# Adding routed expert outputs onto the residual stream in memory, by a scatter with addition

## What is computed

```python
x = x + attention(layer_norm(x))                  # 12 heads of 16
xn = layer_norm(x).reshape(4096, 192)
logits = xn @ gate_w                              # 8 experts
top_logits, top_idx = top_k(logits, 2)
top_gates = softmax(top_logits)                   # two weights for each token
y_e = gelu(xn @ w1[e] + b1[e]) @ w2[e] + b2[e]    # hidden size 768
return x + sum over the two chosen e of gate_e * y_e
```

## Time and profile before

| | us |
|---|---|
| median of 3 runs | 2392.24 |
| lowest and highest | 2391.66, 2395.35 |
| span of the profiled execution | 2403.1 |
| of it, from the first load of the last stage to the end | 29.7 |

### The profile page before, as it was taken

One profiled execution on the slowest core, in us unless ns is written; L12 is line 12 of the kernel. 1 busy time (PEld: TensorE's weight loads), 2 busy tenths in 40 slices (PEclk: granted clock), 3 DMA queues, 4 the chain that ended last, 5 costly groups with the idle time before them and its releaser, 6 DMA issues. The chain is left out here.

```text
span 2403.1 us, 30974 instructions
## 1 busy us (share of the span) xinstructions
PE 1879.3 (78%) x9780; PEld 1007.5 (42%) x9804; DVE 1495.5 (62%) x2518; ACT 1074.7 (45%) x1896; POOL 395.9 (16%) x595
## 2 busy tenths in 40 slices
PE   3868788858876453777668877998899984999994
PEld 2745655535333320000022234442133333888883
DVE  4558449966010687999878876999788883111114
ACT  1100222214110476999979964342477661222220
POOL 5000000000112010222100003331033343222221
PEclk8989999968887575555589978997799996999997
DMA  3011110005797004443011008777666703566664
GB/s 85 1 39 31 48 31 27 20 10 229 309 411 314 20 0 127 127 127 123 18 32 40 26 16 119 130 132 107 83 88 95 97 28 135 195 201 203 202 203 184
DMA packets 147792, 264.98 MB, mean 110 GB/s; under 512 B 28864, under 2 KB 115985, under 8 KB 142678
## 3 DMA queue, kind: packets, MB, share of 16 engines
q1 hardware_dynamic: 135750, 242.10, 38.0%
q0 software_dynamic: 10768, 18.19, 2.3%
q10 hardware_dynamic: 1152, 3.15, 0.3%
HBM read 221.85 MB, written 57.71 MB: 116 GB/s over the span
## 5 line engine op out<-in xcount | busy, mean ns | idle before, releaser
L1743 PE MATMUL ps<-arena 128*128 x376 | 194.9, 621 | 108.2 <-ACT ps L1785 60.1
L1785 ACT ACTIVATE ps<-ps,arena 128x512 f32<-128x512 f32 x384 | 256.7, 1121 | 6.3 <-POOL arena L1769 6.3
L1753 DVE TENSOR_REDUCE arena<-ps 128x1024 f32 x192 | 232.8, 1225 | 24.5 <-PE ps L1743 12.2
L1785 ACT ACTIVATION_READ_ACCUMULATOR ps<-ps,arena 128x1 f32 x384 | 234.7, 668 | 0.0
L2159 DVE TENSOR_REDUCE arena<-ps 128x1024 f32 x192 | 221.3, 1219 | 12.4 <-PE ps L2405 9.8
L2618 ACT ACTIVATE arena<-ps 128x1024 f32<-128x1024 f32 x192 | 185.1, 1020 | 97.6 <-PE ps L2500 96.4
L2962 DVE TENSOR_TENSOR arena<-ps,arena 128x384 f32<-128x384 f32 x39 | 21.8, 558 | 286.4 <-PE ps L2918 286.4
L2942 ACT ACTIVATE arena<-ps,arena 128x256 f32<-128x256 f32 x234 | 89.5, 481 | 235.9 <-PE ps L2907 230.0
L2405 PE MATMUL ps<-arena 96*128 96x512 bf16 x500 | 162.7, 430 | 26.4 <-DVE arena L2159 12.2
L1950 ACT ACTIVATE arena<-ps 128x1024 f32<-128x1024 f32 x192 | 178.7, 1048 | 7.8 <-DVE arena L1970 4.6
L529 PE MATMUL ps<-arena 96*128 96x456 f32 (+1 forms) x512 | 170.3, 482 | 8.8 <-DMA arena<-la_xt 5.2
(11 more groups left out here) (394 smaller groups left out, 3264.8 us busy)
## 6 DMA issues: line engine op xcount, KB each, us to landing
arena<-in_sm_w_dram SPq DMA_DIRECT2D x128, 576.0 KB, 15.5
arena<-in_re_w_dram SPq DMA_DIRECT2D x39, 1252.0 KB, 5.9
arena<-ra_parts SPq DMA_DIRECT2D x192, 192.0 KB, 9.1
routed_in<-routed_in SPq DMA_DIRECT2D x8, 3332.0 KB, 14.2
ra_parts<-arena SPq DMA_DIRECT2D x48, 192.0 KB, 2.4
arena<-routed_in SPq DMA_DIRECT2D x39, 196.0 KB, 5.4
arena<-la_xt SPq DMA_DIRECT2D x16, 384.0 KB, 3.4
arena<-arena SPq DMA_DIRECT2D x64, 96.0 KB, 2.2
```

The lines of the kernel that those rows point to most:

```text
L1743: ins = pe.matmul(ps[:, 2 * (n % 4) + t % 2, :], QM[j][:, h, t * P:(t + 1) * P], KI[:, b, h // HG, :], start=True, stop=True)
L1753: v.tensor_reduce(MXq[:, b, 2 * u:2 * u + 2, at_head(h)], ps[:, 2 * (n % 4):2 * (n % 4) + 2, :], AX.X, ALU.max).then_inc(s_lk, 1)
L1785: ins = act.activation(bank, bank, ACT.Exp, bias=nb[n % 4][:, t % 2:t % 2 + 1], scale=c_reg, accum_out=RS[:, b, t, at_head(h):at_head(h) + 1])
```

## The change

1. The gate weights are made batch by batch. `best_two` also takes the logit gap of its batch (DVE, L2711 of the changed kernel). ACT takes its exponential in `gap_exp(b - 2)`, behind score unit e = 3 of batch b. DVE makes the two weights in `gates`, right behind `places`.
2. `send` copies the weight into word 1 of each row's header on POOL (it waits for `gates`), and word 0 is now the token's own row number, the same for both of its rows.
3. SP stores each batch of the stream `m.H`, as soon as it holds the attention output, into a new DRAM array `routed_sum` (`keep_stream`).
4. In the expert stage DVE also copies the weights from the header, and multiplies `YM` by them with two instructions. POOL's indirect DMAs add onto `routed_sum` instead of storing into `routed_out`.
5. The last stage only copies `routed_sum` to the output, DRAM to DRAM, four copies from SP's and four from ACT's queue. The 16 loads and 64 DVE instructions are gone.

```diff
+            def keep_stream(p):
+                sp.wait_ge(s_hs, p + 1)
+                sp.dma_start(io.routed_sum[p * S:(p + 1) * S].rearrange("(p t) d -> p t d", t=T), m.H[:, p, :, :]
+                             ).then_inc(m.sums_set, 16)
...
+                if b > 2:
+                    keep_stream(b - 3)
...
+            keep_stream(B - 3)
+            keep_stream(B - 2)
             av.wait(sp, B - 1, NS)
...
                 load_rows(sp, io, m, n, at[n])
+            keep_stream(B - 1)
...
+            def gap_exp(p):
+                act.wait_ge(s_d, p + 1)
+                act.activation(gap[p % 2], gap[p % 2], ACT.Exp).then_inc(s_e, 1)
...
+                    if b > 1 and e == 3:
+                        gap_exp(b - 2)
...
+            gap_exp(B - 2)
             turned_copy(B - 1, 0, 0)
             turned_copy(B - 1, 1, 2)
+            gap_exp(B - 1)
...
                 if b and not last:
                     places(b - 1)
+                    gates(b - 1)
...
+                best = VM[:, p * T:(p + 1) * T, :]
+                v.tensor_tensor(gap[p % 2], best[:, :, 1], best[:, :, 0], ALU.subtract).then_inc(s_d, 1)
...
+            def gates(p):
+
+                v.wait_ge(s_e, p + 1)
+                first, second = GT[p % 2][:, 0, :], GT[p % 2][:, 1, :]
+                gate(v.tensor_scalar(second, gap[p % 2], 1.0, None, ALU.add))
+                gate(v.reciprocal(first, second))
+                v.tensor_tensor(second, first, gap[p % 2], ALU.mult).then_inc(s_gt, 1)
...
-                pool.iota(to_row[a], [[1, T]], base=k * NT * P + p * S, channel_multiplier=T).then_inc(s_ir, 1)
-                pool.wait_ge(s_ir, 2 * p + k + 1)
+                pool.iota(to_row[a], [[1, T]], base=p * S, channel_multiplier=T).then_inc(s_ir, 1)
+                pool.wait_ge(s_gt, p + 1)
+                pool.tensor_copy(XA[a][:, :, 1], GT[p % 2][:, k, :]).then_inc(s_ir, 1)
+                pool.wait_ge(s_ir, 2 * (2 * p + k + 1))
...
-                yc.wait(pool, n, 1)
+                yw.wait(pool, n, 1)
...
-                                            YM[j][:, h, :], None).then_inc(m.ym[j], 16)
+                                            YM[j][:, h, :], None, compute_op=ALU.add).then_inc(m.ym[j], 16)
...
+                v.tensor_copy(weight[n % 4], XM[n % 2][:, :, 1])
...
+                yc.wait(v, n, 1)
+                for h in range(2):
+                    ins = v.tensor_scalar(YM[n % 2][:, h, :], YM[n % 2][:, h, :], weight[n % 4][:, h:h + 1], None,
+                                          ALU.mult)
+                ins.then_inc(yw.sem, 1)
...
-                        ins = v.scalar_tensor_tensor(out=m.H[:, b, t, :], in0=Y[:, b, k, t, :],
-                                                     scalar=GT[:, T * b + t, k:k + 1], in1=m.H[:, b, t, :],
-                                                     op0=ALU.mult, op1=ALU.add)
...
+        def copy_out(eng, batches):
+            for b in batches:
+                eng.dma_start(io.out[b].rearrange("(p t) d -> p (t d)", t=T),
+                              yd[b * S:(b + 1) * S].rearrange("(p t) d -> p (t d)", t=T)).then_inc(s_o, 16)
```

More of the change, by code:

```diff
@@ L2031, in routed_attention @@
     m.TE, m.TID = gx(P, [NTILE], I32), gx(P, [NTILE], I32)
-    m.GT, d = gx(P, [B * T, 2]), gx(P, [B * T])
+    GT, gap = [gx(P, [2, T]) for _ in range(2)], [gx(P, [T]) for _ in range(2)]
     to_row = [a.bitcast(I32)[:, :, 0] for a in XA]
@@ L2458, in routed_attention @@
         SG("rows_turned_copied", 2), SG("logits"), SG("logits_copied"), SG("masks"), SG("ranks"), SG("places")
-    s_gl, s_gb, s_ir, s_d, s_e, s_te = (sem(f"ra_gate_{n}") for n in (
-        "chain", "rows_scaled", "return_rows_set", "gap", "gap_exp", "tile_tables"))
+    s_gl, s_gb, s_ir, s_d, s_e, s_te, s_gt, s_hs = (sem(f"ra_gate_{n}") for n in (
+        "chain", "rows_scaled", "headers_set", "gap", "gap_exp", "tile_tables", "gates", "stream_summed"))
     s_sc = [nc.alloc_semaphore(f"ra_rows_sent{k}") for k in range(2)]
@@ L2677, in logits @@
             def logits(p, bank):
-                v.tensor_tensor(m.H[:, p, :, :], m.H[:, p, :, :], X[p % 2], ALU.add)
+                v.tensor_tensor(m.H[:, p, :, :], m.H[:, p, :, :], X[p % 2], ALU.add).then_inc(s_hs, 1)
                 if p == B - 1:
@@ L2742, in _ @@
             places(B - 2)
+            gates(B - 2)
             add_projection(B - 1, (7, 3), True)
@@ L2749, in _ @@
             places(B - 1)
+            gates(B - 1)
             gate(v.tensor_tensor(row0, row0, part0, ALU.subtract))
@@ L2768, in _ @@
             v.tensor_scalar(m.TID, TG, float(NX * PART), None, ALU.min).then_inc(s_te, 1)
-            v.tensor_tensor(d, VM[:, :, 1], VM[:, :, 0], ALU.subtract).then_inc(s_d, 1)
-            v.wait_ge(s_e, 1)
-            gate(v.tensor_scalar(m.GT[:, :, 1], d, 1.0, None, ALU.add))
-            gate(v.reciprocal(m.GT[:, :, 0], m.GT[:, :, 1]))
-            gate(v.tensor_tensor(m.GT[:, :, 1], m.GT[:, :, 0], d, ALU.mult))
         @block.gpsimd
@@ L2837, in routed_experts @@
 def routed_experts(nc, m, io):
-    ps, GT, WR, wl = m.ps, m.GT, m.WR, m.wl
-    xd, yd = io.routed_in, io.routed_out
+    ps, WR, wl = m.ps, m.WR, m.wl
+    xd, yd = io.routed_in, io.routed_sum
     sem = lambda name: SEMS.new(nc, name)
@@ L2845, in routed_experts @@
     XM, XT, HT, YM = m.XM, two([2, TR]), two([KH, TR]), two([2, D])
-    back = [w(P, [2], I32) for _ in range(4)]
+    back, weight = [w(P, [2], I32) for _ in range(4)], [w(P, [2]) for _ in range(4)]
     xm = m.xm
@@ L2849, in routed_experts @@
     S2 = lambda n, per=1: Signal(nc, f"re_t_{n}", per, 2 * per)
-    xt, xc, hp, gl, yp, yc, yf = S2("rows_turned"), S2("rows_turned_copied"), S2("hidden", 3), S2("gelu", 3), \
-        S2("out"), S2("out_copied"), S2("out_buffer_free")
+    xt, xc, hp, gl, yp, yc, yw, yf = S2("rows_turned"), S2("rows_turned_copied"), S2("hidden", 3), S2("gelu", 3), \
+        S2("out"), S2("out_copied"), S2("out_weighted"), S2("out_buffer_free")
     unit = lambda k: ps[:, 1 + k, 0:TR]
@@ L2948, in _ @@
             yc.start(v)
+            yw.start(v)
             def rows(n):
```

35 lines of the change are left out of this document (9 added, 26 removed).

## The result

| | before | changed |
|---|---|---|
| median, us | 2392.48 | 2417.72 |
| lowest and highest, 4 runs each | 2391.66, 2395.35 | 2411.17, 2423.11 |
| span of the profiled execution | 2403.1 | 2409.4 |

The ratio is 1.0094, 95% interval 1.0075 to 1.0113: 22.5 us slower (18 to 27), or 25.2 by the medians. The forecast was 2398.4 with a range up to 2412. The sign was right and the size was not.

The account below looks back on a forecast made before the run. PE and DVE, both near full, were taken to bound the attention loop by hand-overs, PE the expert loop, and DVE sums the last stage. 14.6 + 3.6 + 1.8 - 13.8 = +6.2 us gave 2398.4 us; range 2392 to 2405, wider 2386 to 2412.

Parts of the forecast that it names:

- ACT's wait: Attention loop, behind unit 3: ACT waits for DVE's gap in six batches, making the kernel 14.6 us slower in sum.
- PE's clock: Rival, attention loop: PE's clock falls in the new pauses, adding 9.9 us, to 2408.3; chance 0.14.
- The rival's price: Attention loop, clock rival: 2.15 us more for a batch at low clock, 9.9 us in all; chance 0.14.
- Gates: Attention loop, DVE between the ranks and step 8: three small instructions, 0.6 us a batch, 3.6 us loss.
- The offset between profile and median: Whole kernel: the profiled execution was 10.9 us over the median before, taken as the same after.
- Free wait (rival): Attention loop: batches settle with MAX8 ahead of unit 3, the wait costs nothing, 2385.0 us; chance 0.14.
- Between the stages: Between attention and expert loops: last gap and gates, POOL's copies and last stream store lose 1.8 us, ends 0.8 and 3.
- Expert loop: Expert stage: DVE's 0.8 us more in each tile is hidden and landing may grow by 5.7 us, so no loss.
- Tail: Last stage: 8 DRAM to DRAM copies of 13.0 us replace loads and DVE sums, gain 13.8 us, ends 7.7 and 17.9.

Follow-up runs that it names:

- E9: The changed kernel with fourteen matmuls that nobody reads put into TensorE's pause behind unit 3: ratio 1.0070 to the kernel before, six batches 227.4 us.
- E10: The changed kernel, exponential still behind unit 3, with only the gates moved into VectorE's idle time: ratio 1.0062 to the kernel before, six batches 225.8 us.
- E4: The changed kernel without gap subtraction, exponential, gates and weight copy, so expert outputs are unweighted: ratio 0.9933 to the kernel before, six batches 203.3 us.
- E2: The changed kernel with the exponential behind unit 7 and the gates moved into VectorE's idle time: ratio 0.9928 to the kernel before, tail 21.3 us.
- E7: E2 with GpSimd's scatters storing instead of adding, which changes the computation: ratio 0.9922 to the kernel before, tail 18.3 us.
- E8: E2 with stream and experts' rows put straight into the output, padding beyond the scatter's bound, no last stage: ratio 0.9895 to the kernel before.
- E1: The changed kernel with ScalarE's small exponential moved from behind unit 3 to behind unit 7: ratio 0.9968 to the kernel before, six batches 206.1 us.
- E3: The kernel before plus only the gap subtraction and its exponential behind unit 3, result unused: ratio 1.0060 to the kernel before, six batches 226.2 us.
- E5: The changed kernel with ScalarE's small exponential behind unit 5 instead of unit 3: ratio 0.9975 to the kernel before, six batches 211.7 us.
- E6: The changed kernel with eight matmuls that nobody reads put into TensorE's pause behind unit 3: ratio 1.0043 to the kernel before, six batches 230.4 us.

## Why the prediction was wrong, step by step

- **ACT's wait: right.** Foreseen 3.6 us late in four batches, 3.2 and 3.6 in the others; measured 3.9 in six. The rest is that the exponential starts behind the gap. The price that the forecast derived by following the queue, 2.9 us a batch, is 2.8 in the batches at full clock of E9 and 3.1 in that of E10.
- **PE's clock: the step that failed.** The forecast carried the wait through at the speed of the kernel before ("when PE alone sets the pace") and kept the low clock as a rival with a chance of 0.14 and a price of 9.9 us. The runs take the 34.8 us apart: E4, which has neither wait nor gates, has 203.3 us for the six batches, 2.2 less than the kernel before (E2, E7 and E8 have the same loop and spread over 4 us, so each of these numbers is good to some 2); gates add 2.8 (E1, 206.1); the bare wait adds 6 x 2.8 = 17; and the 17 that are left up to 240.3 are half clock (19.5 if counted as 240.3 - 6 x 36.8). The forecast named alone, and there the low clock did not follow a pause: PE had stood for no more than 0.3 us in the 8 us before. The row that bears on a pause stands elsewhere in the kernel before, in its timeline of PE at 735 us:

```profile
734.97 0.88 PE L1259 MATMUL ps<-arena 4*128 4x384 f32 x2 [3.55 <-issue]
735.77 0.85 PE L1262 MATMUL ps<-arena 128*32 128x384 f32 x8
736.56 1.64 PE L1259 MATMUL ps<-arena 4*128 4x384 f32 x2
```

Behind 3.55 us of idleness two matmuls of L1259 take 0.88 us, and the next two of the same line, at half clock, 1.64 us; the granted clock is 1.00 before, 0.62 from 736 to 738 us and 0.50 behind. The same happens behind a pause of 3.19 us at 758.75. Against that, all pauses in step 8 of the kernel before (1.57 to 1.75 us) left the clock full. With the forecast's own arithmetic, by which PE would stand for some three microseconds more in each batch, the rival deserved more than 0.14.

- **The rival's price: too low.** It took 2.15 us from one stretch of the kernel before and one such stretch in a batch. In the change each of the last four batches has two, behind unit 3 and in step 8, together 41.0 - 36.8 = 4.2 us. A single stretch cost less than the rival said, 1.4 to 1.6 us (batches 2 and 3 of the change against 36.8); two in one batch cost more than twice that.
- **Gates: right in size, wrong as a separate term.** Their 0.6 us a batch cost 0.4 to 4.3 us in six batches where there is no wait (E1 against E7, E8, E4 and E2; 2.8 against the mean of E2, E7 and E8), 3.6 foreseen. Beside the wait they cost 14.5 us (E10), because they lengthen a pause of PE, the one in step 8, behind which five of six batches then ran at half clock. Two costs that were added as if they were independent were not: E3, 20.6 us, and the gates' 3.6 do not make 34.8.
- **The offset between profile and median: an assumption that failed.** The profiled execution before was 10.9 us above the median and the forecast took the same after. It was 8.3 below (2409.4 and 2417.72), and that the span of 2409.3 forecast for it was met is luck. In the untouched part ahead of the first score exponential, the eleven profiled executions of the other kernels, which are alike there, needed 1692 to 1707 us and that of the kernel before 1709: it was the slowest. This did not change the forecast, which used differences, but a comparison of the two spans alone would have confirmed it wrongly.
- **Free wait (rival): wrong.** The batches did not settle with MAX8 ahead of unit 3; six of six waited. In E5, with unit 5, the wait shrank to a third of a microsecond in two batches but did not vanish in any.
- **Between the stages: 1.1, foreseen 1.8.** Ends 0.8 and 3.
- **Expert loop: right.** 323.5 us in each kernel. The landings of the adding scatter took 6.0 us at the median (those before have no row), and five tiles waited for one without delaying the loop.
- **Tail: right in sum, not in its parts.** 13.0 against 13.8. The copies took 12.7 us to the end of the span, where 13.0 and 1.2 behind them were set. The adding scatter cost 3.0 us (E7) where 1.0 was taken and 2.0 was its end. From the last bias add to the last tile's first issue it is 3.0 us in E2 and 1.4 in E7, since the landing of the tile before is waited for (the 3.08 us ahead of the issue at 2391.05): 1.6. The two issues are 1.2 longer (1.55 for 0.97 each), the landing some 0.5, and the copies behind it took 0.2 less. The forecast had priced the last landing alone. The two errors are of opposite sign, so that the sum came out right is in part luck.
- **The forecast's own range: a slip.** From the ends of the tail and the gates it is 2393.7 to 2405.7, not 2392 to 2405; this changes nothing above.

What stays open: why the clock falls behind a pause in one batch and not in the next. Behind unit 3 all pauses of 3.1 us in the change, E3 and E10 were followed by slow matmuls (16 of 16) and none of the 1.5 us ones (2 of 2), but in E6 two pauses of 1.4 us were, and four weren't. In step 8 a pause of 2.0 to 2.2 us is harmless in five of six batches of E1 and followed by half clock in five of six of the change, and in E7 one of 1.68 us was followed by it too. So the length of the pause is not all; the busy time of PE before it was not varied by itself. The clock had just been low ahead of both 1.5 us pauses, at the end of the batch before, and it also falls where there is no pause: in the kernel before at 1869.7 us, in the change at 1791.4 us. That the pause behind unit 3 brings the low clock is shown by E9, in one profiled execution; why step 8 kept full clock in five batches of E1 and in only one of the change, at pauses of the same length, is not.

## What to carry to other kernels

A wait that a small instruction puts into the queue of the engine that paces the loop can be paid twice: once in time, and once in the clock of the matrix engine that then stands still. Here the two parts were of about the same size, 17 us each. So the place of the instruction comes first: one that nobody needs soon belongs far behind its producer, and three small ones belong where their engine idles. And before a rival "the clock falls" is given a small chance, count the new idle time of TensorE in each round of the loop; several small costs that all lengthen one pause are not to be added up one by one.

## What the runs showed of the chip

- An indirect DMA with addition takes GpSimd 1.55 us to issue and without it 0.97 us, at 78 each (E2 and E7), and it made the tail 3.0 us longer.
- TensorE behind a pause of 3.1 us ran at 1.2 GHz for 6 us in the change (granted clock 0.50 in three rows), for instructions that take 1.7 to 1.8 times as long then. Matmuls that nobody reads, put into the pause, held the clock at that place: fourteen of them in six batches of six, eight in four of six (E9, E6).
- Indices beyond the bound of an indirect scatter were left out at no visible cost (E8), so that padding needs no rows of its own to go to.
- Copies of 3.15 MB from DRAM to DRAM on two queues took 12.7 us up to the end of the span, where the padding copies' price gave 13.0 and 1.2 behind them.
